# Attention: queries, keys, values and the turned x side by side in a step

## What is computed

```python
q = (x @ Wq).reshape(B, S, 16, 64)      # B = 8 batches, S = 512, x is B x S x 128
k = (x @ Wk).reshape(B, S, 16, 64)
v = (x @ Wv).reshape(B, S, 16, 64)
scores = einsum('bqhd,bkhd->bhqk', q, k) / 8 + bias
attn = softmax(scores)
ctx = einsum('bhqk,bkhd->bqhd', attn, v).reshape(B, S, 1024)
x = layernorm(x + ctx @ Wo)
```

## Time and profile before

| what | us |
|---|---|
| median of three runs (lowest, highest) | 1984.38 (1983.81, 1985.91) |
| the profiled execution: time | 1987.07 |
| its span, first to last instruction | 1985.1 |
| TensorE busy in the span | 1676.8 |
| VectorE, ScalarE, POOL busy | 1395.0, 1174.5, 703.4 |

### The profile page before, as it was taken

One profiled execution on the slowest core, in us unless ns is written; L12 is line 12 of the kernel. 1 busy time (PEld: TensorE's weight loads), 2 busy tenths in 40 slices (PEclk: granted clock), 3 DMA queues, 4 the chain that ended last, 5 costly groups with the idle time before them and its releaser, 6 DMA issues. The chain is left out here.

```text
span 1985.1 us, 39441 instructions
## 1 busy us (share of the span) xinstructions
PE 1676.8 (84%) x13628; PEld 1252.5 (63%) x13628; DVE 1395.0 (70%) x3853; ACT 1174.5 (59%) x2786; POOL 703.4 (35%) x666
## 2 busy tenths in 40 slices
PE   8999999999999999973875779999899988933871
PEld 5666666666666666662764448887688867722761
DVE  6777777777777778856756757777678767668324
ACT  6777777777777777753554656665466634521323
POOL 0122221221122112211656308996388921000672
PEclk9999999999999999995987979999999999965886
DMA  6000000000000000031754000000000000050444
GB/s 237 2 2 2 1 2 1 2 2 2 2 2 1 2 2 2 2 94 14 127 129 101 23 0 1 1 1 1 1 1 1 1 1 5 3 158 0 122 84 98
DMA packets 63895, 61.14 MB, mean 31 GB/s; under 512 B 10682, under 2 KB 53668, under 8 KB 63572
## 3 DMA queue, kind: packets, MB, share of 16 engines
q1 hardware_dynamic: 51236, 40.98, 6.8%
q0 software_dynamic: 10384, 16.59, 5.2%
q10 hardware_dynamic: 2080, 1.05, 0.2%
HBM read 39.60 MB, written 18.73 MB: 29 GB/s over the span
## 5 line engine op out<-in xcount | busy, mean ns | idle before, releaser
L167 POOL TENSOR_TENSOR x<-x,scaled 128x512 f32<-128x512 f32 x128 | 165.5, 1293 | 704.0 <-DVE scaled L464 694.9
L443 DVE CUSTOM_DVE_ANT_0 prob<-score_ps,bias 128x512 f32<-128x512 f32 x512 | 345.4, 684 | 69.0 <-issue 69.0
L369 ACT ACTIVATE prob<-prob,negmax 128x512 f32<-128x512 f32 x512 | 365.9, 725 | 0.5 <-DVE negmax L443 0.5
L239 PE MATMUL score_ps<-k,q 64*128 64x512 f32 x1536 | 251.7, 434 | 6.0 <-DVE q L423 5.2
L354 ACT COPY probT<-turn_ps 128x512 f32<-128x512 f32 x256 | 150.4, 588 | 156.8 <-PE turn_ps L254 156.8
L270 PE MATMUL work_ps<-probT,val 128*64 128x512 f32 x1024 | 233.8, 598 | 0.0
L254 PEld LDWEIGHTS turn_ps<-ident,prob 64*128 64x128 f32 x4096 | 171.3, 141 | 39.6 <-ACT probT L354 3.1
L239 PEld LDWEIGHTS score_ps<-k,q 64*128 64x128 f32 x1536 | 128.3, 190 | 96.3 <-issue 75.1
L451 DVE COPY probT<-turn_ps 128x512 f32<-128x512 f32 x256 | 175.7, 686 | 4.0 <-PE turn_ps L254 3.9
L254 PE MATMUL turn_ps<-ident,prob 64*128 64x64 f32 x4096 | 171.5, 224 | 2.5 <-DVE probT L451 2.3
L270 PEld LDWEIGHTS work_ps<-probT,val 128*64 128x64 f32 x1024 | 67.6, 136 | 114.2 <-issue 90.3
(11 more groups left out here) (511 smaller groups left out, 4099.2 us busy)
## 6 DMA issues: line engine op xcount, KB each, us to landing
ew<-L_ffn_fc_weight SPq DMA_DIRECT2D x32, 256.0 KB, 3.3
bias<-bias_line SPq DMA_DIRECT2D x16, 448.0 KB, 7.7
mid_rows<-row SPq DMA_DIRECT2D x40, 128.5 KB, 4.4
last_rows<-row SPq DMA_DIRECT2D x40, 64.0 KB
rows_dram<-qk SPq DMA_DIRECT2D x1, 2304.0 KB, 18.7
x_rows<-x SPq DMA_DIRECT2D x4, 512.0 KB, 6.4
acc_dram<-zero POOLq DMA_DIRECT2D x1, 2048.0 KB, 16.3
out<-x SPq DMA_DIRECT2D x4, 512.0 KB, 3.2
```

Of the source, the lines that this page charges most:

```text
L167: pool.tensor_tensor(mine, mine, scaled[a][:, :, :], ALU.add).then_inc(added, 1)
L239: mm = pe.matmul(score_ps[i % 2][a][:, :], q[p % 2][u][head(a), tile_of(i)], k[p % 2][v][head(a), :], start=(n == 0), stop=(n == 2))
L369: act.activation(mine, mine, ACT.Exp, bias=negmax[p % 2][:, i, a:a + 1], scale=-1.0, accum_out=total[p % 4][:, i, a:a + 1]).then_inc(exp_d ...
L443: dve.tensor_tensor_reduce(prob[p % 2][a][:, i, :], score_ps[i % 2][a][:, :], bias[:, h, first:first + SEQ][:, ::-1], -1.0, 3.0e38, ALU.ad ...
```

## The change

`values` now go into `turn_ps[0]` and the turned x into `turn_ps[1]`, the banks of the turns; `queries` take `work[1]`, `keys` and the context `work[0]`. On TensorE queries, turned x, keys and values of pair s+1 stand behind each other between turn(s-1, 1) and scores(s, 3). Values are made one step earlier than before, the last of a pair's four contexts and its add_heads later. The waits follow the banks: queries wait for the scaled heads of the pair four before, keys for the copied context of the pair three before, values for VectorE's copy and turned x for ScalarE's copy of turn 1, turn 2 for the copied values (and x's low part), add_heads for the low parts of the next queries and keys. ScalarE and VectorE take the two turn banks in alternation, and their steps have a new order. VectorE's first score of a pair waits for the last turn of the pair two before. At the start `queries` come ahead of `keys`, and the values of pair 0 ahead of the first scores. No instruction's shape changes.

```diff
         def _(pe):
             def turn_rows(b):
                 for j in range(QT):
-                    mm = pe.transpose(work[0][:, tile_of(j)], x[:, b * QT + j, :], ident[:, :])
+                    mm = pe.transpose(turn_ps[1][:, tile_of(j)], x[:, b * QT + j, :], ident[:, :])
...
-            def turn_next_rows(s):
-                if turns_x(s):
-                    pe.wait_ge(q_lo, s + 2)
+            def turn_next_rows(p):
+                if turns_x(p):
+                    pe.wait_ge(turned_by_act, QT * (p - 1) + 2)
                     pe.wait_ge(x_in, 16)
-                    turn_rows(batch_of(s) + 1)
+                    turn_rows(batch_of(p) + 1)
...
-            def keys(p):
+            def queries(p):
                 if is_pair(p):
                     if p % PAIRS == 0:
                         pe.wait_ge(x_lo, batch_of(p) + 1)
+                    if p >= 4:
+                        pe.wait_ge(scaled_ready, 2 * (p - 4) + 2)
+                    elif p >= 1:
+                        pe.wait_ge(q_lo, p)
+                    if p in (0, 2):
+                        pe.wait_ge(w_lo, 1 if p == 0 else 4)
+                    project(work[1], wq, p, q_done)
+
+            def keys(p):
+                if is_pair(p):
                     if p >= 3:
-                        pe.wait_ge(scaled_ready, 2 * (p - 3) + 2)
+                        pe.wait_ge(ctx_ready, p - 2)
                     elif p >= 1:
                         pe.wait_ge(k_lo, p)
                     if p in (0, 2):
                         pe.wait_ge(w_lo, 2 if p == 0 else 5)
-                    project(work[1], wk, p, k_done)
-
-            def queries(p):
+                    project(work[0], wk, p, k_done)
+
+            def values(p):
+
                 if is_pair(p):
-                    if p >= 3:
-                        pe.wait_ge(scaled_ready, 2 * (p - 3) + 1)
-                    elif p >= 1:
-                        pe.wait_ge(val_ready, p)
-                    if p == 2:
-                        pe.wait_ge(w_lo, 4)
-                    project(work[0], wq, p, q_done)
-
-            def values(p):
-
-                if is_pair(p):
-                    if turns_x(p - 1):
-                        pe.wait_ge(x_lo, batch_of(p) + 2)
-                    else:
-                        pe.wait_ge(q_lo, p + 1)
+                    if p >= 2:
+                        pe.wait_ge(turned_by_dve, QT * (p - 2) + 2)
+                    elif p == 1:
+                        pe.wait_ge(val_ready, 1)
                     if p in (0, 2):
...
-                            mm = pe.matmul(work[0][:, t * GW:(t + 1) * GW], xs[u][:, tile_of(first + t)], wv[v][:, group * GW:(group + 1) * GW],
+                            mm = pe.matmul(turn_ps[0][:, t * GW:(t + 1) * GW], xs[u][:, tile_of(first + t)], wv[v][:, group * GW:(group + 1) * GW],
...
+                    if c == 0 and p == 0:
+                        pe.wait_ge(val_ready, 2)
+                    if c == 2 and is_pair(p + 2):
+                        pe.wait_ge(val_ready, p + 3)
+                    if c == 2 and turns_x(p + 1):
+                        pe.wait_ge(x_lo, batch_of(p + 1) + 2)
...
                     if c == 0:
-                        if p + 2 < STEPS:
-                            pe.wait_ge(k_lo, p + 3)
+                        if p == 0:
+                            pe.wait_ge(k_lo, 3)
                         else:
-                            pe.wait_ge(scaled_ready, 2 * p)
+                            pe.wait_ge(scaled_ready, 2 * p - 1)
                         if p % 2 == 0:
                             pe.wait_ge(val_ready, p + 2)
...
-                        mm = pe.matmul(work[1][head(a), :], val[p // 2 % 2][:, c, p % 2 * 2 + a, :], probT[:, c, a, :], start=(c == 0), stop=(c == QT - 1))
+                        mm = pe.matmul(work[0][head(a), :], val[p // 2 % 2][:, c, p % 2 * 2 + a, :], probT[:, c, a, :], start=(c == 0), stop=(c == QT - 1))
...
                     pe.wait_ge(ctx_ready, p + 1)
-                    if p + 2 < STEPS:
-                        pe.wait_ge(val_ready, p + 3)
+                    if is_pair(p + 3):
+                        pe.wait_ge(k_lo, p + 4)
+                        pe.wait_ge(q_lo, p + 4)
                     else:
-                        pe.wait_ge(scaled_ready, 2 * p - 1)
+                        pe.wait_ge(scaled_ready, 2 * p)
...
             def step(s):
+                context(s - 2, 3)
                 turn(s - 1, 0)
-                values(s)
                 scores(s, 1)
+                scores(s, 2)
                 turn(s - 1, 1)
+                queries(s + 1)
+                turn_next_rows(s)
+                keys(s + 1)
+                values(s + 1)
+                scores(s, 3)
+                turn(s - 1, 2)
                 add_heads(s - 2)
-                scores(s, 2)
-                turn(s - 1, 2)
-                keys(s + 1)
-                queries(s + 1)
-                scores(s, 3)
+                scores(s + 1, 0)
                 turn(s - 1, 3)
-                for c in range(QT):
+                for c in range(3):
                     context(s - 1, c)
-                turn_next_rows(s)
-                scores(s + 1, 0)
 
...
-                act.copy(xT[b % 2][0][:, :], work[0][:, :]).then_inc(x_hi, 1)
+                act.copy(xT[b % 2][0][:, :], turn_ps[1][:, :]).then_inc(x_hi, 1)
...
-                    act.copy(q[p % 2][0][:, :], work[0][:, :]).then_inc(q_hi, 1)
+                    act.copy(q[p % 2][0][:, :], work[1][:, :]).then_inc(q_hi, 1)
...
-                    act.copy(k[p % 2][0][:, :], work[1][:, :]).then_inc(k_hi, 1)
+                    act.copy(k[p % 2][0][:, :], work[0][:, :]).then_inc(k_hi, 1)
...
-                             work[0][:, :].rearrange("p (t h d) -> p t h d", t=2, h=GROUP)).then_inc(val_ready, 1)
+                             turn_ps[0][:, :].rearrange("p (t h d) -> p t h d", t=2, h=GROUP)).then_inc(val_ready, 1)
...
-                    act.copy(turned(c, 0), of_bank(0)).then_inc(turned_by_act, 1)
+                    act.copy(turned(c, c % 2), of_bank(c % 2)).then_inc(turned_by_act, 1)
...
-                    act.copy(ctxT[:, :], work[1][:, :]).then_inc(ctx_ready, 1)
+                    act.copy(ctxT[:, :], work[0][:, :]).then_inc(ctx_ready, 1)
...
             def step(s):
-                copy_context(s - 2)
-                copy_next_rows(s - 1)
-                copy_values(s)
-                turn(s - 1, 1)
-                exps(s, 0, 0)
-                exps(s, 0, 1)
-                exps(s, 1, 0)
-                copy_k(s + 1)
-                turn(s - 1, 2)
-                copy_q(s + 1)
-                exps(s, 1, 1)
                 exps(s, 2, 0)
                 exps(s, 2, 1)
+                exps(s, 3, 0)
                 turn(s - 1, 3)
-                exps(s, 3, 0)
                 exps(s, 3, 1)
+                exps(s + 1, 0, 0)
                 turn(s, 0)
+                exps(s + 1, 0, 1)
+                copy_context(s - 1)
+                turn(s, 1)
+                exps(s + 1, 1, 0)
+                copy_q(s + 2)
+                copy_next_rows(s + 1)
+                copy_k(s + 2)
+                copy_values(s + 2)
+                exps(s + 1, 1, 1)
+                turn(s, 2)
...
-            for s in range(-1, STEPS + 2):
+            for s in range(-2, STEPS + 2):
                 step(s)
-                if s == -1:
+                if s == -2:
                     high_parts(4)
                     high_parts(5)
...
+                        if p >= 2 and i == 0:
+                            dve.wait_ge(turn_done, QT * (p - 1))
...
-                    dve.tensor_copy(turned(c, 1), of_bank(1)).then_inc(turned_by_dve, 1)
+                    dve.tensor_copy(turned(c, 1 - c % 2), of_bank(1 - c % 2)).then_inc(turned_by_dve, 1)
...
             def step(s):
-                score(s - 1, 2, 1)
-                score(s - 1, 3, 0)
-                turn(s - 2, 3)
-                score(s - 1, 3, 1)
-                rest_of_q(s)
-                rest_of_next_rows(s - 1)
+                rest_of_k(s + 1)
+                score(s, 2, 1)
+                turn(s - 1, 2)
+                scale_head(s - 2, 0)
+                score(s, 3, 0)
+                scale_head(s - 2, 1)
+                turn(s - 1, 3)
+                score(s, 3, 1)
+                score(s + 1, 0, 0)
+                score(s + 1, 0, 1)
                 invert(s - 1)
-                score(s, 0, 0)
-                turn(s - 1, 0)
-                score(s, 0, 1)
-                score(s, 1, 0)
-                turn(s - 1, 1)
-                scale_head(s - 2, 0)
-                scale_head(s - 2, 1)
-                score(s, 1, 1)
-                turn(s - 1, 2)
-                score(s, 2, 0)
-                rest_of_k(s + 1)
+                turn(s, 0)
+                score(s + 1, 1, 0)
+                score(s + 1, 1, 1)
+                turn(s, 1)
+                score(s + 1, 2, 0)
```

(33 more changed lines are left out.)

## The result

The kernel after takes 1921.96 us (median of four runs, 1916.29 to 1922.59), the kernel before 1985.14 in the same comparison. The ratio is 0.9669 with a 95% interval of 0.9654 to 0.9684, so it is 3.3% faster, by 63 us. A second comparison gave 0.9666 (0.9651 to 0.9681). The prediction said 1920. The profiled executions, on which all block times rest, took 1987.07 and 1921.56 us, 65.5 apart.

The account below looks back on a forecast made before the run. TensorE's own sequence and its holes were taken to bound the kernel. Steady steps 35.4 us, turns of x 28.9 and the ends 0 summed to 64 us saved, giving 1920 us, range 1908 to 1944.

Parts of the forecast that it names:

- (a): Plain step, scores(0) to scores(0): 12.08 us instead of 12.66, 35.4 us over 61 steps.
- The 0.35 forecast for joins: Per step, 0.35 of 0.63 us gained at transitions between blocks, as between 64-row and 128-row work on TensorE.
- (b): Waits in the new order: turn(2) tightest with 0.03 us in hand, add_heads with 0.28 to spare.
- the 0.05 that was charged: At turn(2), 0.05 us a step for weights loaded later because of the wait for the copied values.
- rival 4: At add_heads, a ring of waits through three engines becomes the bound: costs 71 us, 1991 us; chance 0.07.
- (c): Seven turns of x, now between queries and keys: 0.5 us each instead of 4.63, 28.9 us gained.
- (d): Ends of the attention stage: 3 us gained at the start, 2.8 lost at the end, sum about 0.
- Joins that aren't saved: Block transitions stay as costly; only the hole at keys and turns of x gain: 21 us back, 1941; chance 0.12.
- Rival 2: At turn(2), values copied 0.3 us late in each step: 18 us back, 1938 us; chance 0.12.
- rivals 3 to 5: Turning x still rests TensorE: 14 us, 0.06; rival 4; another wait cancels the gain: within 0.2%, 0.03.

Follow-up runs that it names:

- the two experiments: Kernel after, ScalarE's exp(1, 1) ahead of the values' copy: 1956.22 us; kernel after, VectorE's score(2, 1) ahead of k's low part: 1940.44 us.
- the fill: Kernel before, with 18 transposes of the identity on TensorE where values wait for the turned x, instead of resting: 1977.82 us, 0.9954.
- the run with them back: Kernel after, with VectorE making the low parts of all weights ahead of the first q, as before the change: 1926.41 us, 0.9705.
- the kernel without the hole: Kernel before, with the second head scaled and added for only 128 of 512 queries, so keys find work[1] free sooner: 1962.82 us, 0.9873.
- the third visit: Kernel after, queries ahead of turn(1), so three visits to 128 rows a step: 1981.12 us; with ScalarE's copy of q also moved ahead: 1956.06 us.

## Why the prediction was right, point by point

**The steady step (a).** 12.08 was forecast, 12.09 came. The blocks at unseen joins: turn(0) 0.52 (taken 0.57, within its bounds), scores(1) and (2) together 1.48 (1.48), values 0.80 (0.79). turn(2) and turn(3) took 0.52 and 0.61, each 0.03 more than taken. The sizes of these errors are small and of both signs. The 0.35 forecast for joins came as 0.30, and it was no single thing: 0.20 in the projections' blocks, from the visit saved, and 0.10 from the two scores behind each other.

**What waits (b).** The order of tightness was right: turn(2), then add_heads. scores(3) to turn(2) takes 0.84 for 0.80, and its weight load starts late, the 0.05 that was charged; the two experiments priced both places. The ring of rival 4 had some 0.3 us in hand, as counted (0.28), and never used it.

**Turning x (c).** 0.5 a turn was forecast and 0.55 came, 28.9 against 28.5 us. That the clock fell because TensorE rested, on which part of the sum lay, was shown by the fill: without the rest it stayed up in seven of seven turns.

**The ends (d).** Here two sizes were off. The start gave 6.6 and not 3 us. The moved low parts are 3.66 of these at pair 2 (the run with them back has its scores(0) at 36.59). That run has two stretches of slow clock at the start (0.53 from 18 to 21, 0.50 from 29 to 31), as the kernel before has, and the kernel after only one, so a stretch of slow clock is part of the 3.66. The other 2.95 no run takes apart; that the first steps are shorter in the new order is part of them. The end took 3.8 and not 2.8. Of these 2.95 are the counted part: turn(0) of the last pair starts 14.64 us behind its scores(0), where I had 14.5 against 11.69. The other 0.85 lie behind it, where the last turns rest and the granted clock falls to 0.50 (793 to 796 us); before, it stayed at 1.00 there (856 to 868 us):

```profile
790.36 0.72 PE L260 MATMUL turn_ps<-ident,prob 64*128 64x64 f32 x16 [0.88 <-DVE probT L461]
791.96 0.72 PE L260 MATMUL turn_ps<-ident,prob 64*128 64x64 f32 x16 [0.88 <-DVE probT L461]
792.47 1.96 PE L292 MATMUL work_ps<-wo,ctxT 64*128 64x128 f32 x16
```

The gain at the start lies outside its bounds of 0 and 5, the loss at the end inside those of 1 and 5; together they gave 2.8 us where 0 was forecast. That the median came within 2 us of 1920 is in part luck: by the traces attention gained 66.5 us and not 64, the layers behind took 1 us back, and the runs of the kernel after spread over 6 us.

**The rivals.** Joins that aren't saved (1941 us) is refuted by the step itself, by the 12.39 us of the kernel without the hole, and by the third visit. The extra visit cost 0.36 us. The Trainium skill, TensorE: Matmul & The Clock Gate, Step-by-step: what each phase is for, says that weight loads are pulled ahead of running matmuls; the trace agrees only where the block ahead uses the array in the same way. Behind queries, on 128 rows, the first weight load of the scores starts together with their first matmul (at 445.73), while the turns behind the scores, 64 rows both, have theirs loaded 0.23 ahead (446.30, the first turn at 446.53). The weight loads of the kernel before:

```profile
445.73 0.53 PEld L239 LDWEIGHTS score_ps<-k,q 64*128 64x128 f32 x6 [0.36 <-issue]
446.30 0.74 PEld L254 LDWEIGHTS turn_ps<-ident,prob 64*128 64x128 f32 x16
```

The Trainium skill, TensorEngine Tiling (Array Packing), Key Properties, says that changing the tiling mode drains the engine, and the late loads fit that. That each join is such a drain is the skill's account; the runs show the late load and the price only. Rival 2's condition arose only to the 0.05 us charged; its price was right, since the delay put there on purpose was paid in full. Those of rivals 3 to 5 didn't arise: no turn of x made TensorE rest, though turn(2) came 0.11 late behind each.

## What to carry to other kernels

Where one engine is busy throughout, write its order as a row of blocks, take from the trace what each costs in front of its neighbour, and add up the new order; then lay the other in-order queues against it and look for the least slack. Group work that uses the array in the same way: one visit to 128 rows more cost 0.36 us a step here, one fewer saved 0.20. A short rest of TensorE may cost more than its length: behind 2.4 us of rest the slow clock cost another 1.56. So either move the work behind cover, or fill the rest.

## What the runs showed of the hardware that I had not expected

Whether a rest lowers the clock isn't decided by its length alone. The same rest of 2.4 us behind the turned x was followed by the lower clock in 7 of 7 cases in the kernel before, and in 2 of 7 in the kernel without the hole of 0.28 us; why those two, no run tells. Of the 2 of 7, the first, in the windows of that kernel:

```profile
396.00:399.00 3.00, 1.32 (x22) 1.00 (x22) 0.04 (x1) 1.56 (x3) 0.00 (x0) 1.00 0.00 0
399.00:406.00 7.00, 6.29 (x48) 5.57 (x50) 4.32 (x13) 2.76 (x7) 0.00 (x0) 0.51 0.00 0
```

Here the granted clock is 0.51 over 7 us, longer than in the earlier trace rows, and the step takes 17.63 us, where a plain one takes 12.39 and one with the same rest and the full clock 14.84. At the end of the stage in the kernel after, the clock fell behind two rests of 0.88 us. In the kernel before, eighteen plain transposes of the identity in place of the rest were enough to keep the clock up in all seven cases.
